# A hybrid layer on one core: the numerators of batch 0 on two PSUM banks, and new order lists for every pass

## The reference, cut to what matters

```python
q, k = elu(q) + 1, elu(k) + 1
weights = (rot(q) @ rot(k).T) / (q @ k.T)        # numerator / denominator, 512 x 512 per head
x = x + (weights @ v) @ w_out + b_out            # attention
x = x + ffn(norm(x))                             # top 2 of 8 experts and a shared one, 128 -> 512 -> 128
x = x + mamba(norm(x))                           # h = dA * h + dt * B * x, 16 states, 256 channels, 512 steps
x = x + ffn(norm(x))
```

## Time and profile before

| | us |
|---|---|
| median of 3 runs | 3860.93 (3859.01 to 3870.79) |
| the profiled execution | 3871.34 |
| its span, first to last instruction | 3869.4 |
| PE busy in the span | 3456.1 (89%) |
| ACT busy | 3236.8 (84%) |
| DVE busy | 2746.1 (71%) |
| POOL busy | 1277.1 (33%) |
| table loads on ACT, 554 | 710.8 |
| FIRST, from 76 to 199 | 123 |

### The profile page before, as it was taken

One profiled execution on the slowest core, in us unless ns is written; L12 is line 12 of the kernel. 1 busy time (PEld: TensorE's weight loads), 2 busy tenths in 40 slices (PEclk: granted clock), 3 DMA queues, 4 the chain that ended last, 5 costly groups with the idle time before them and its releaser, 6 DMA issues. The chain is left out here.

```text
span 3869.4 us, 38405 instructions
## 1 busy us (share of the span) xinstructions
PE 3456.1 (89%) x11446; PEld 1442.6 (37%) x11446; DVE 2746.1 (71%) x3513; ACT 3236.8 (84%) x4060; POOL 1277.1 (33%) x758
## 2 busy tenths in 40 slices
PE   3787699999999999999999999999999999998857
PEld 1131243434344343434444343434434343344424
DVE  2426667777686877878686777868687787868692
ACT  2667589998998989999998989999898999887663
POOL 1102243423233342423334242323334242314261
PEclk9586699999999999999999999999999999999978
DMA  4142336445354545436363644535454544534332
GB/s 147 46 136 61 117 123 184 143 148 160 121 174 131 176 138 178 152 122 195 116 185 123 179 148 140 168 122 175 142 169 133 185 145 134 179 99 160 122 127 101
DMA packets 214848, 552.02 MB, mean 143 GB/s; under 512 B 25105, under 2 KB 96626, under 8 KB 214642
## 3 DMA queue, kind: packets, MB, share of 16 engines
q1 hardware_dynamic: 214642, 549.57, 45.7%
HBM read 488.65 MB, written 63.18 MB: 143 GB/s over the span
## 5 line engine op out<-in xcount | busy, mean ns | idle before, releaser
L783 PE MATMUL bank<-hF,wst 128*128 128x512 f32 x2304 | 1171.9, 625 | 25.3 <-DVE tmp L1180 20.8
L1110 DVE TENSOR_TENSOR rPool<-bank,rPool 128x512 f32<-128x512 f32 x1024 | 703.1, 687 | 559.7 <-PE bank L713 514.1
L885 ACT ACTIVATE hF<-bank,cols 128x512 f32<-128x512 f32 x1152 | 770.9, 686 | 253.9 <-PE bank L774 245.5
L1330 POOL TENSOR_TENSOR yM<-yM,ws 128x1024 f32<-128x1024 f32 x240 | 595.1, 2479 | 1026.1 <-DVE ws L1229 1023.7
L1023 ACT ACT_TABLE_LOAD x554 | 710.8, 1283 | 9.7
L885 ACT ACTIVATE rPool<-bank 128x512 f32<-128x512 f32 x1024 | 571.2, 596 | 162.4 <-PE bank L708 156.9
L772 PE MATMUL bank<-xnH,wst 128*128 128x512 f32 x1152 | 599.5, 520 | 68.5 <-DMA wst<-wscr 36.4
L1222 DVE TENSOR_TENSOR_SCAN ws<-dAs,ws 128x1024 f32<-128x1024 f32 x256 | 635.5, 2487 | 6.9 <-ACT dAs L885 5.5
L1315 POOL TENSOR_TENSOR acc<-acc,tmp 128x512 f32<-128x512 f32 x240 | 353.1, 1471 | 835.7 <-DVE tmp L1180 827.3
L783 PEld LDWEIGHTS bank<-hF,wst 128*128 128x128 f32 x2304 | 412.7, 193 | 434.4 <-issue 347.7
L713 PE MATMUL bank<-qpk,kpk 48*128 48x512 bf16 x1024 | 420.3, 410 | 122.6 <-DVE rPool L1110 122.0
(11 more groups left out here) (157 smaller groups left out, 2948.4 us busy)
## 6 DMA issues: line engine op xcount, KB each, us to landing
wst<-wscr SPq DMA_DIRECT2D x288, 768.0 KB, 5.5
bc<-bcscr SPq DMA_DIRECT2D x256, 512.0 KB, 4.9
cB<-gscr SPq DMA_DIRECT2D x256, 256.0 KB, 4.8
qscr<-parts SPq DMA_DIRECT2D x192, 128.0 KB, 2.2
kscr<-parts SPq DMA_DIRECT2D x192, 128.0 KB, 3.7
kpk<-kscr SPq DMA_DIRECT2D x128, 192.0 KB, 6.0
qpk<-qscr SPq DMA_DIRECT2D x128, 192.0 KB, 6.5
wscr<-wst SPq DMA_DIRECT2D x9, 512.0 KB, 2.9
```

The lines of the kernel that those rows point to most:

```text
L783: pe.matmul(ps[FFN][:, :], w2, hF[:, (NCH * f + q) % HSLOTS, :], start=(c == 0), stop=(c == FC - 1)).then_inc(s_dn, 1)
L885: return nc.scalar.activation(out_, in_, fn, **kw)
L1110: v.tensor_tensor(rP[:, slot, c, :], ps[NUM][:, :], rP[:, slot, c, :], ALU.mult).then_inc(s_mul, 1)
L1330: g.tensor_tensor(yM[:, :, :], yM[:, :, :], ws[:, s % 3, :, :], ALU.add).then_inc(s_ya, 1)
```

## The change

Numerators of batch 0 go to NUM when their number is even and to bank FFN when it is odd, and each waits for the multiply two before it. The multiply reads the same bank. The first `down` of the first FFN waits until all 64 multiplies of batch 0 are done. All other batches keep one bank. The order lists of all passes are replaced. In HEAD the first cast comes before the third `P.qk`. In FIRST all casts come before `A.oT`, `P.keep` is POOL's last, and the last `W.store` are ahead of the last `P.pk`. In SECOND the last casts also come before `A.oT`; it has 20 table loads instead of 24, LAST has 48 instead of 50, MAIN 34 as before. The numbers of all other operations are the same.

```diff
     "ACT": """
-    P.load P.mean P.var P.qk*4 P.cast*8
+    P.load P.mean P.var P.qk*2 P.cast P.qk P.cast*3 P.qk P.cast*4
...
     "POOL": """
-    P.keep P.rope P.rest*4 P.rope P.rest*4
+    P.rope P.rest*4 P.rope P.rest*3 P.keep P.rest
 FIRST = {
     "SP": """
-    P.in W.store*7 A.load*2 P.pk*4 P.ahead*2 W.store*2
+    P.in W.store*5 A.load W.store A.load P.pk*2 W.store*3 P.pk*2 P.ahead*2
...
     "PE": """
-    A.den A.num A.den*3 A.v A.den*2 P.load A.num A.den P.mean A.num A.den*2 A.num A.den A.num A.av P.var A.den
-    A.num*2 A.den*2 A.num P.qk A.num A.av A.num A.den*2 A.num A.den*2 A.num P.qk A.num A.av A.den A.num A.den*2
-    A.num A.den*2 A.num*2 A.av A.num A.den*2 A.num P.qk A.num*2 A.den A.av A.num A.den*3 A.num*2 P.qk A.den A.num
-    A.av A.den A.num A.den A.num A.den*2 A.num*2 A.av A.den A.num A.den*2 A.num*3 A.den A.av A.num A.den*2 A.num
-    A.den*2 A.num*2 A.av A.num A.den*3 A.num A.den A.num*2 A.av A.num A.den*3 A.num*3 A.den A.av A.num A.den*3
-    A.num*2 A.den*2 A.num A.av A.num A.den*2 A.num A.den A.num*2 A.av A.num A.den*3 A.num A.den A.num*2 A.den A.av
-    A.num A.den A.num A.den A.num*2 A.av A.num*3 A.av A.close
+    A.den A.num*2 A.den*3 A.v A.den*2 P.load P.mean A.num A.den A.num A.den P.var A.av A.num A.den A.num*2 A.den*4
+    A.num P.qk A.den A.num A.av A.den A.num*2 A.den P.qk A.num A.den*2 A.num*2 A.av A.num A.den*2 P.qk A.den*2
+    A.num*2 A.av A.num*3 A.den*3 P.qk A.num A.den A.num*2 A.den A.av A.den*2 A.num*2 A.den*2 A.av A.num A.den*3
+    A.num A.den A.num*3 A.av A.den*2 A.num*2 A.den*2 A.num A.den A.av A.den*2 A.num*2 A.den A.num A.den A.num A.den
+    A.num A.den A.num A.av A.num A.av A.den A.num A.den*5 A.num A.den A.num*2 A.av A.num A.den A.num*4 A.av A.num
+    A.den A.num A.den*2 A.num A.den A.av A.num*2 A.den*3 A.num A.den A.num A.av A.den*2 A.num*4 A.av A.num*4 A.av
+    A.close
 """,
     "ACT": """
-    A.ln*4 A.ex A.ln P.load A.ln*3 A.ex P.mean A.ln*2 P.var A.ln*2 A.ex P.qk A.ln*4 A.ex A.ln*4 A.ex P.qk A.ln*4
-    A.ex P.qk A.ln*4 A.ex P.qk A.ln*4 A.ex P.cast A.ln*4 A.ex A.ln*4 A.ex A.ln*4 A.ex P.cast A.ln*4 A.ex P.cast
-    A.ln*4 A.ex A.ln*4 A.ex P.cast A.ln*4 A.ex A.ln*4 A.ex P.cast*3 A.oT P.cast
+    A.ln*4 A.ex P.load A.ln*4 P.mean A.ex P.var A.ln*4 A.ex A.ln P.qk A.ln*3 A.ex A.ln P.qk A.ln*3 A.ex P.qk A.ln*4
+    A.ex P.qk A.ln*7 A.ex A.ln*3 A.ex P.cast A.ln*2 A.ex A.ln*4 P.cast A.ex A.ln*4 A.ex A.ln*2 P.cast A.ln*6 P.cast
+    A.ex*2 P.cast*2 A.ln*4 P.cast A.ex A.ln*5 P.cast A.ln A.ex A.ln*2 A.ex A.oT
 """,
     "DVE": """
-    W.split*2 A.v W.split A.mul*3 P.mean A.mul W.split A.mul W.split A.mul*2 P.var A.mul W.split A.mul*4 W.split
-    A.mul*4 W.split A.mul*4 P.til A.mul P.til A.mul P.til A.mul*6 W.split A.mul*4 P.til A.mul*32 A.close
+    W.split*4 A.v A.mul W.split A.mul*2 P.mean A.mul*4 P.var A.mul*2 P.til A.mul*4 W.split P.til A.mul*6 W.split
+    A.mul W.split*2 A.mul P.til*2 A.mul*43 A.close
...
     "POOL": """
-    P.rope*2 P.rest*7 P.keep P.rest
+    P.rope P.rest P.rope P.rest*7 P.keep
 """,
 }
...
 SECOND = {
     "SP": """
-    F.w P.in F.w*3 F.rows F.gate*2 F.w*2 F.gate*2 F.w*2 F.gate F.w F.gate*3 A.load M.rows M.bc*2 A.load P.pk M.bc*5
-    P.pk*3 P.ahead*2
+    P.in F.w*4 F.rows F.gate*2 F.w*2 F.gate*3 F.w*2 A.load F.gate F.w F.gate*2 P.pk M.rows A.load M.bc*3 P.pk M.bc*3
+    P.pk*2 M.bc P.ahead*2
...
     "ACT": """
-    A.ln*3 F.mean A.ln*2 F.var A.ex T.gelu F.gelu*4 T.log A.ln*2 F.router A.ln A.ex A.ln*2 T.gelu F.gelu*2 T.log
-    A.ln*2 P.load A.ex T.gelu F.gelu*4 P.mean F.gelu*4 T.log P.var A.ln*4 T.gelu F.gelu*3 T.log A.ln*2 P.qk A.ex
-    T.gelu F.gelu*3 T.log A.ln T.gelu F.gelu*4 T.log A.ln T.gelu F.gelu*6 T.log P.qk A.ex T.gelu F.gelu*3 T.log
-    A.ln*3 T.gelu F.gelu*3 T.log P.qk P.cast A.ln P.qk A.ex M.mean P.cast A.ln M.var A.ln*2 M.xp P.cast A.ln M.xp
-    A.ex M.xp T.silu M.silu M.xp M.silu T.log A.ln*2 M.row P.cast A.ln*2 M.dt A.ex M.dt M.sp A.ln*4 A.ex M.decay*2
-    A.ln*2 T.silu M.silu T.log A.ln*2 M.decay A.ex A.ln M.decay A.ln*3 A.ex T.silu M.silu T.log A.ln*4 A.ex M.decay
-    A.ln*4 M.decay A.ex A.ln M.decay P.cast A.ln*3 A.ex A.ln*4 A.ex A.ln*4 P.cast A.ex A.oT P.cast*2
+    A.ln*2 F.mean F.var A.ln*4 A.ex F.router T.gelu F.gelu*4 T.log A.ln*2 A.ex T.gelu F.gelu*2 T.log A.ln P.load
+    A.ln*3 A.ex T.gelu F.gelu*5 P.mean F.gelu*3 T.log P.var A.ln*4 T.gelu F.gelu*3 T.log P.qk A.ex T.gelu F.gelu*6
+    T.log A.ln*4 T.gelu F.gelu*6 T.log A.ex P.qk T.gelu F.gelu*5 T.log A.ln*2 T.gelu F.gelu*2 T.log A.ln*2 P.qk
+    P.cast P.qk A.ex M.mean M.var A.ln P.cast M.xp A.ln*2 M.xp A.ln A.ex M.xp T.silu M.silu*2 M.xp T.log A.ln M.row
+    A.ln*2 P.cast A.ln M.dt A.ex A.ln*2 P.cast A.ln M.dt M.sp A.ln A.ex A.ln*4 M.decay A.ex A.ln*3 M.decay*2 A.ln
+    A.ex P.cast A.ln*4 M.decay A.ex T.silu M.silu*2 T.log A.ln*4 A.ex A.ln*6 P.cast M.decay*2 A.ex A.ln P.cast A.ln
+    A.ex A.ln M.decay P.cast A.ln*3 A.ex A.oT
 """,
...
     "POOL": """
-    F.add*5 P.rope F.add*2 M.take P.rest*4 P.rope M.acc*3 M.keep M.acc P.rest*3 M.acc P.rest P.keep M.acc
+    F.add*4 P.rope F.add*3 P.rest M.take M.keep P.rest P.rope P.rest*2 M.acc P.rest*4 M.acc*3 P.keep M.acc*2
 """,
...
 MAIN = {
     "SP": """
-    N.bc*2 H.w P.in H.gate F.w H.gate N.bc*2 F.rows F.w H.out N.bc F.gate F.w*2 N.bc*3 F.gate F.w*2 A.load N.bc
-    F.gate*2 F.w F.gate F.w F.gate F.w F.gate P.pk G.w F.gate G.rows G.gate*2 G.w*2 M.rows G.w A.load P.pk M.bc*4
-    G.w G.gate M.bc G.w*2 P.pk G.gate M.bc*2 P.pk G.gate P.ahead G.gate G.w P.ahead
+    N.bc*2 H.gate H.w H.gate F.w P.in F.w N.bc*2 H.out F.rows N.bc F.w F.gate N.bc F.gate*2 F.w N.bc*2 F.w N.bc F.w
+    A.load F.w F.gate*3 F.w F.gate*2 F.w P.pk G.w*2 G.rows P.pk*2 G.gate*2 G.w M.rows M.bc A.load M.bc*2 G.w*2
+    M.bc*2 G.w G.gate*2 P.pk M.bc*2 G.w P.ahead*2 G.w G.gate*2
 """,
...
 LAST = {
     "DVE": """
-    F.mean N.dbx H.part N.scan N.hc N.dbx H.part N.scan N.dbx N.hc H.part F.var F.router N.dbx H.part N.scan F.route
...
-    M.scan M.dbx M.hc G.part M.scan M.hc M.dbx M.scan M.dbx M.hc M.scan G.part M.hc M.dbx M.scan M.hc M.dbx G.part
-    M.scan M.dbx M.hc M.scan G.part M.dbx M.scan M.hc*2
+    H.part F.mean N.dbx N.scan N.dbx H.part N.hc N.scan H.part N.hc F.var N.dbx N.scan H.part F.router N.dbx F.route
...
+    M.dbx M.hc M.scan G.part M.hc M.dbx G.part M.dbx M.scan*2 G.part M.hc*2 M.dbx*2 M.scan*2 M.hc*2 G.part M.dbx*2
+    M.scan M.hc M.scan M.hc
...
@@ -502,6 +503,9 @@
         def heads(i):
             return min(i + 1, NB) if isinstance(i, int) else i + 1
 
+        def num_bank(b, n):
+            return FFN if b == 0 and n % 2 else NUM
+
         def outs_before(i):
             return floor(i - 2)
 
@@ -709,8 +713,8 @@
                 else:
                     if n == 0:
                         pe.wait_ge(s_x1_done, floor(b))
-                    pe.wait_ge(s_mul, floor(UNITS * b + n))
-                    pe.matmul(ps[NUM][:, :], lhs, rhs, start=True, stop=True).then_inc(s_num, 1)
+                    pe.wait_ge(s_mul, floor(UNITS * b + n - (b == 0)))
+                    pe.matmul(ps[num_bank(b, n)][:, :], lhs, rhs, start=True, stop=True).then_inc(s_num, 1)
 
             def att(b, name, s):
                 if name == "v":
@@ -774,6 +778,8 @@
                     pe.matmul(bank, high, xnH[:, :], start=False, stop=True).then_inc(s_up, 1)
                 elif name == "down":
                     e, c = divmod(q, FC)
+                    if q == 0 and f == 0:
+                        pe.wait_ge(s_mul, UNITS)
                     if q == 0:
                         pe.wait_ge(s_out_c, floor(outs))
                     if c == 0:
@@ -1107,7 +1113,7 @@
                         v.wait_ge(s_ex, floor(STEPS * b + step + 1))
                     v.wait_ge(s_num, floor(UNITS * b + s + 1))
                     slot = (STEPS * b + step) % RSLOTS
-                    v.tensor_tensor(rP[:, slot, c, :], ps[NUM][:, :], rP[:, slot, c, :], ALU.mult).then_inc(s_mul, 1)
+                    v.tensor_tensor(rP[:, slot, c, :], ps[num_bank(b, s)][:, :], rP[:, slot, c, :], ALU.mult).then_inc(s_mul, 1)
                 elif name == "close":
                     v.wait_ge(s_oproj, floor(b + 1))
                     v.wait_ge(s_keep, floor(b + 1))
```

155 lines of the change are left out of this document (78 added, 77 removed).

## The result

The changed kernel takes 3899.4 us (median of four runs, 3883.6 to 3905.4), the kernel before beside it 3860.0 (3853.7 to 3870.8): ratio 1.0095, interval 1.0072 to 1.0117. It is slower by 39 us, where I had forecast 70 less, and 3899 lies outside my range.

What follows compares the result with a forecast made beforehand. It took FIRST as bound by the one-bank PE-DVE loop, MAIN by PE and ACT near their limits, plus idle seams. From the profiled 3871.3 us, -1 -22 -15 -12 -3 -14 -3 = -70, less 10.4, gave 3791 us; range 3750 to 3840.

Steps and rivals of the forecast that it cites:

- HEAD, -1: HEAD: first cast before the third P.qk starts casts and remainders 2 us earlier; gain 0 to 2, taken 1 us.
- FIRST, -22: Batch 0's attention: two banks loosen the numerator-multiply loop, 97 to 100 us instead of 122; taken -22 us.
- the order binding as before in most steps, -9: FIRST's smallest-gain bound: order still binds most steps, only the loop part goes (1.39 to 1.2 on 48 units), -9 us.
- Rival 2: FIRST: PE's denser work brings 2.4 GHz, ACT's 82 us then limits; another -10 us, 3781; chance 0.10.
- Rival 1: FIRST: PE's order, not the bank, binds; -9 there, perhaps -8 at seam 1, 3811 us; chance 0.12.
- Seam 1, -15: Between FIRST and SECOND: earlier last cast lands batch 1's k tile about with xFin, F.mean follows by 2; -15 us.
- SECOND's inside, -3: Inside SECOND: four table loads fewer on ACT, more PE units; taken -3 us (-8 to +4).
- Seam 2, -12: Between SECOND and MAIN: earlier last casts, F.mean about 6 us after xFin instead of 17.9; -12 us (-6 to -14).
- MAIN, -1.0 a pass: MAIN's 14 passes: PE saves 1.6, ACT's gelu waits 1.4, partly hidden; -1.0 us a pass, -14 in all (-42 to +21).
- rival 4: MAIN: H.w behind H.gate in SyncE's queue delays weights and ups; at 5 us a pass +70, 3875 us; chance 0.03.
- LAST and END, -3: LAST and END: a scan covers one POOL addition (2.3 us), two table loads fewer; taken -3 us (-8 to +3).
- Rival 5: Second bank covers batch 0 alone, 64 of 1024 numerators, so its gain can't exceed FIRST's; no chance given.

Runs made afterwards that it cites:

- e5: Kernel before with only the second bank for batch 0's numerators added, every order list old: 3830.8 us.
- e10: e8 with PE's and DVE's FIRST lists of the kernel before, and ACT's old FIRST list with its casts earlier: 3788.6 us.
- e11: e10 with one token moved in LAST's DVE list, the M.hc of step 14 ahead of the last M.dbx: 3786.9 us.
- e12: e2 with the last 27 tokens of LAST's DVE list rewritten so that each step runs M.dbx, M.scan, M.hc in turn: 3824.2 us.
- e6: e1 with FIRST's last P.cast put back behind A.oT in ACT's list: 3825.7 us.
- e1: Changed kernel with the MAIN, LAST and END lists of the kernel before; second bank and HEAD to SECOND stay new: 3810.9 us.
- e2: Changed kernel with MAIN's five lists of the kernel before; LAST and END stay new: 3819.9 us.
- e4: Changed kernel with MAIN's SP list rewritten, weight loads moved directly ahead of gate loads that need a later event: 3846.3 us.
- e3: Changed kernel with MAIN's SP list of the kernel before: 4061.4 us.
- e7: e1 with MAIN's SP list of the change, the other MAIN lists old: 3930.5 us.
- e9: e4 with MAIN's PE and ACT lists of the kernel before: 4350.5 us.
- e8: e1 with three tokens moved in MAIN's old SP list (F.w 4, P.in, F.w 5): 3796.6 us.

## Why the prediction was wrong, step by step

**HEAD, -1:** measured -1.0 (denominator 0 at 74.8).

**FIRST, -22:** the size is near, -19.2, but not the reason. I took the new list as the one that lets the second bank pay and PE at 1.2 GHz throughout. e5 shows -30.4 with the old list, and the new list giving 11 of it back. Two terms were off. The bound "the order binding as before in most steps, -9" rested on a wrong reason: with the old order it was mainly the bank that held PE. And the clock does rise: numerators and denominators of FIRST in after, eight of them from 138.18 to 140.55, last 0.39 us, which is 2.4 GHz, where before had 0.60 to 0.61. Rival 2, to which I gave 0.10, is real as a mechanism: 53 of the 128 matmuls of FIRST ran at full clock in after and 66 in e5, against 8. What it is worth no run isolates. With the same lists of FIRST, e10 and e11 took 93.1 and 92.2 us with 52 and 64 such matmuls, e12 and after 106.0 and 103.3 with 35 and 53, so 0.08 to 0.15 us each; by that the clock gave an estimated 3 to 7 of the 19 us of after, 4 to 9 of the 30 of e5. That -19.2 lies near -22 is luck: the list took back what the bank and the clock gave beyond my sum.

Rival 1, that PE's order and not the bank binds, is refuted by e5, where the order is the old one and FIRST is 30 us shorter. The Trainium skill's page TensorE: Matmul & The Clock Gate (HAM oscillation — how this bites in real kernels) reports a kernel to which PSUM double-buffering gave no further gain; the rows spoke against that here, and e5 measures it: 30 us of 122, what the clock gave included. The same page warns (A second HAM failure mode: psum-queue depth-cycling) that going round the banks costs the clock; here the granted clock rose (0.64 to 0.78 in e5).

**Seam 1, -15, and SECOND's inside, -3:** right. `F.mean` follows xFin by 1.8 us instead of 15.5, the first up by 10.7 instead of 27.2, -16.5, and -1.6 remain for SECOND's inside. e6 shows the main cause, the place of the last cast.

**Seam 2, -12:** the step held and another wait took part of it.

```profile
384.92 2.04 PE L678 MATMUL bank<-xFin,onesD 128*128 128x512 f32 x2 [0.33 <-DVE vpad L1106]
...
390.48 2.28 DVE L1228 TENSOR_TENSOR_SCAN ws<-dAs,ws 128x1024 f32<-128x1024 f32 x1
...
394.10 2.34 POOL L1336 TENSOR_TENSOR yM<-yM,ws 128x1024 f32<-128x1024 f32 x1 [9.19 <-DVE ws L1235]
...
394.54 4.05 DVE L1228 TENSOR_TENSOR_SCAN ws<-dAs,ws 128x1024 f32<-128x1024 f32 x1
...
400.46 0.77 PE L776 MATMUL bank<-xnH,wst 128*128 128x512 f32 x1 [9.50 <-issue]
```

`F.mean` follows xFin(1) by 6.3 us instead of 18.7, -12.4. But in the new PE list F.up 0 stands directly behind `F.var` in this pass (H's entries are left out in it), ahead of the router, and there PE waits 9.5 us for xnH and xnL, which DVE makes behind a scan of 4.05 us. The stretch to xFin(2) gained 8.4 instead of 13. With the old MAIN, e1 and e2 gain 15.5 and 18.1 in it.

**MAIN, -1.0 a pass:** this is the step that failed. It gave +3.85 a pass in the profiles, +50.0 over the 13. Its first half, PE's saving of 1.6, looks right by the number, 1.7, but by luck: some 17 of the 19.9 us in twelve passes are the higher granted clock, which leaves about 0.2 a pass for the fewer slots and the fewer changes between kinds of matmul that I had counted. The second, ACT's gelus waiting 1.4 less, had the wrong sign: ACT's wait for ups rose from 144.8 to 188.6 us in twelve passes, and with the weights in time (e4) it is still 163.9 (after, then e4):

```profile
ACT hF L891 <- PE bank L778: 188.6, 284, 4.0
```

```profile
ACT hF L891 <- PE bank L778: 163.9, 277, 4.5
```

The sentence that was false is "No list shows a place that must cost more". SP's list showed it: F.w 3 behind the second and third gate, F.w 8 behind the seventh and eighth. I had described the mechanism as rival 4, for one load, H.w, and had argued it away with "gate and load need the same four `H.down`". They don't wait for the same thing: the load of weights e+1 waits for the downs of expert e-2 on PE, the gate load e for the part that DVE makes from them, when its list comes to it. Behind a gate a load is late by DVE's list, up to 24 us here; it lands after 6 us more, and only the time until its first up hides it. By the table the ups paid for F.w 0, behind the second H.gate, and for F.w 3, and both waits are gone in e4. G.w 6, as late in e4 as in after, is another case and stays. e4 prices the orders of SyncE's list: 40 us of twelve passes' 47. H.w itself, the load that I had named, was 4.0 us late and no up waited for it. The chance of 0.03 was far too low: MAIN lost 3.85 us a pass against before and 4.0 against e2, where the threshold was 4.0.

I had counted the entries of the lists for PE and ACT, and had not laid the events that SP's entries wait for beside those of DVE. Rows for it were at hand: in before SP stood 599 us at weight loads, which says that most of them leave as soon as their slot is free.

**LAST and END, -3:** measured +9.2. By the marks of the trace, 4.6 lie ahead of the scan chain of batch 15 (first dbx 144.9 instead of 140.3 after xFin(15)), 3.2 in it (111.1 instead of 107.9), 1.4 behind it. The two ends of POOL that I wanted to cover were worth 0.5 us at most (e11), because DVE and POOL slow each other where they overlap. That the chain lost by the late bc loads is not borne out by e12; what its 3 us are, and the 4.6 ahead of it, stays open.

**Rival 5,** that the bank covers batch 0 alone, is true, and the bank's own gain, 29 us in e5, lies in FIRST.

## What to carry to other kernels

- In a queue served in order, sort the entries by the event that each waits for, as the other engines' lists produce them. Put a load whose slot is freed by one engine ahead of an entry that waits for a second engine's answer to the same work, and look in the trace at what the queue stood in front of.
- Lists that were made together are one object. Change one only with its partners' events at hand, and measure a new mechanism (here the second bank) on the old lists first: it was worth 29 us there, and the new lists hid that some of their parts lost.

## What the runs showed of the hardware that I had not expected

- PE's stalls can go with a lower clock and then cost more than their length. With the change's list for PE, PE was idle 178 us in twelve passes in e4 and 210 in after, both at a granted clock of 0.99, and 276 in e3 at 0.96; with the list of before 139 in e1 at 0.98, 218 in e7 at 0.97 and 418 in e9 at 0.92. Busy time for the same matmuls was 2482, 2490 and 2567, and 2503, 2523 and 2678 us. More than half of e3's loss against after, 77 of 143 us, is busy time. The sum of the idle time doesn't decide it: after and e7 idle nearly the same, at 0.99 and 0.97.
- PE's busy time is no measure of its work where the clock moves: before, after and e4 show 2510, 2490 and 2482 us in twelve passes. With the busy time inside half-clock stretches counted half it is 2463, 2460 and 2460 us, and in e1, e2, e3, e7, e8 and e9 it lies between 2454 and 2462.
- In FIRST fewer stalls at the bank went with a higher clock: 66 of 128 matmuls at full clock in e5, 8 in before.
- DVE and POOL hold each other up. The scan takes 2.28 us alone and 4.05 when it starts 0.44 us after an addition of 2.34 (the rows at seam 2), about the rest of that addition and a scan; its mean over 16 is 3.34 beside POOL's additions and 2.62 where the order keeps them apart; the addition takes 2.34 alone and 4.3 beside a scan or an hc. The Trainium skill says so too (SBUF — State Buffer, Terms: a port pair that the two engines take exclusively for a full instruction), and these numbers agree with it.
